# Convolution and attention kernel: another order, other engines and other buffers in the prologue

## The reference, cut to what matters

```python
def gn(v): ...  # 32 groups of 8 channels: (v - mean) / sqrt(var + 1e-5)
p = gn(x).mean((2, 3))
angle = tanh(relu(p @ ap_w1.T + ap_b1) @ ap_w2.T + ap_b2) * pi / 4
mod = sigmoid(relu(p @ meta_w1.T + meta_b1) @ meta_w2.T + meta_b2)
x = x + conv3x3(gn(x), rotate(base_kernel, angle)) * mod
t = gn(x) as tokens
q, k, v = t @ Wq.T + bq, t @ Wk.T + bk, t @ Wv.T + bv
q, k = focus((relu(q) + 1e-6) / softplus(scale)), the same of k  # cubes with the norm kept
out = q (k.T v) / (q . sum k) + dwconv5x5(v) + dwc_b           # per head
x = x + out @ Wproj.T + bproj
```

## Time and profile before

| what | us |
|---|---|
| median of three runs | 3972.8 |
| the profiled execution | 3968.21 |
| its span (first to last instruction) | 3966.1 |
| TensorE busy in the span | 3555.9 (90%) |
| VectorE, ScalarE, GpSimd busy | 2978.9, 2704.6, 1425.3 |
| first convolution starts on TensorE | 113.67 |
| second convolution starts on TensorE | 198.11 |
| first `squares` of the loop over images | 286.17 |

### The profile page before, as it was taken

The page is one execution under the profiler, slowest core; times in us unless marked ns, Lnnn a source line. Parts: engine busy times, 40 slices in busy tenths (PEclk is TensorE's granted clock), DMA queues, the critical chain, the costliest instruction groups (busy, mean ns, idle before and its releaser), DMA issues.

```text
span 3966.1 us, 96093 instructions
## 1 busy us (share of the span) xinstructions
PE 3555.9 (90%) x27980; PEld 2859.5 (72%) x27980; DVE 2978.9 (75%) x8235; ACT 2704.6 (68%) x7348; POOL 1425.3 (36%) x1318
## 2 busy tenths in 40 slices
PE   0569989999999999999999998999999899999797
PEld 0138777777877777777777877777787777778686
DVE  6766877868778786877868687786868778585756
ACT  2247776776777677677766767776677767677675
POOL 4532442514334252433525243351424425140302
PEclk9989999999999999999999999999999999999999
DMA  4672634536354452635436263443636344260302
GB/s 156 202 236 65 173 98 143 161 90 186 109 155 116 131 173 82 184 112 149 130 111 192 71 184 113 138 141 108 179 91 178 99 145 132 79 181 22 102 17 75
DMA packets 560047, 516.42 MB, mean 130 GB/s; under 512 B 97600, under 2 KB 491968, under 8 KB 559552
## 3 DMA queue, kind: packets, MB, share of 16 engines
q1 hardware_dynamic: 555200, 508.99, 43.4%
q10 hardware_dynamic: 4352, 1.57, 0.2%
HBM read 351.06 MB, written 134.22 MB: 122 GB/s over the span
## 4 chain that ended last, share of the span: by engine, by line
PE 34%; DVE 29%; issue 17%; ACT 14%; DVEq 2%; DMA 1%; ACTq 1%; SPq 1%; POOL 1%; POOLq 0%
PE F L1557 7%; ACT K L1295 6%; PE VAB L1557 6%; PE F L1518 6%; PE VAB L1518 5%; PE T L1529 4%; DVE F L975 3%; DVE XR L1064 3%; ACT K L1301 3%; DVE XR L1057 3%; DVE XHL L969 3%; DVE K L981 2%; DVE XR L1046 2%; DVE RATIO L989 2%; PE PP L1608 2%
## 5 line engine op out<-in xcount | busy, mean ns | idle before, releaser
L1518 PE MATMUL F<-WQ,XHL 128*128 128x256 f16 x6144 | 819.3, 274 | 27.7 <-ACT V L1335 19.1
L650 POOL TENSOR_TENSOR XR<-XR,V 128x512 f32<-128x512 f32 x256 | 325.6, 1272 | 1042.9 <-DVE XR L1046 1042.9
L1518 PEld LDWEIGHTS F<-WQ,XHL 128*128 128x128 f16 (+1 forms) x6144 | 602.2, 99 | 106.8 <-issue 33.9
L1301 ACT ACTIVATE K<-K,SCAL 128x256 f32<-128x256 f32 x1024 | 512.4, 505 | 209.2 <-DVE K L981 208.2
L634 POOL TENSOR_TENSOR SL<-PL,SL 128x1122 f16<-128x1122 f32 x112 | 259.7, 2319 | 1065.2 <-DVE SL L947 1065.2
L1504 PE MATMUL SM<-SL,BD 128*128 128x512 f16 x2688 | 634.9, 385 | 0.0
L1295 ACT ACTIVATE K<-F,SCAL 128x256 f32<-128x256 f32 x1024 | 473.4, 469 | 232.0 <-DVE F L975 231.6
L975 DVE TENSOR_TENSOR F<-F,FL 128x512 f32<-128x512 f32 x512 | 354.1, 692 | 176.7 <-PE F L1520 175.4
L981 DVE TENSOR_TENSOR K<-K,F 128x512 f32<-128x512 f32 x512 | 349.3, 682 | 167.2 <-ACT K L1295 166.6
L1504 PEld LDWEIGHTS SM<-SL,BD 128*128 128x128 f16 x2688 | 261.0, 97 | 284.1
L1608 PE MATMUL PP<-XR,WP 128*128 128x256 f16 x3072 | 385.6, 276 | 67.8 <-DVE XR L1064 67.8
(11 more groups left out here) (194 smaller groups left out, 6948.0 us busy)
## 6 DMA issues: line engine op xcount, KB each, us to landing
XR<-xr SPq DMA_DIRECT2D x132, 512.0 KB, 5.2
U<-x SPq DMA_DIRECT2D x256, 256.0 KB, 3.8
XR<-x SPq DMA_DIRECT2D x256, 256.0 KB, 4.1
out<-XR SPq DMA_DIRECT2D x256, 256.0 KB, 3.8
PL<-xp SPq DMA_DIRECT2D x112, 561.0 KB, 3.8
RX<-xr SPq DMA_DIRECT2D x118, 512.0 KB, 4.2
x<-RX SPq DMA_DIRECT2D x448, 128.0 KB, 2.1
BD<-RX SPq DMA_DIRECT2D x240, 96.0 KB, 2.2
```

The lines of the kernel that those rows point to most:

```text
L650: g_.tensor_tensor(o, o, fm, ALU.add).then_inc(o_rdy, 2)
L1301: a.activation(K2[:, p, t * C:(t + 1) * C], K3[:, p, t * C:(t + 1) * C], ACT.Square, scale=inv_a, accum_out=S6[:, 2 * p + t:2 * p + t + 1] ...
L1518: t_.matmul(o, XHL[:, xa, h, at], WQ[:, wa, h, c0:c0 + C], start=(k == 0), stop=False)
```

## The change

- **SP's order**: the pixels of image 0 first, then the convolution's constants, then planes, the scale, four tiles of image 1, and only then the taps' scalars and the attention's weights. `load_stats(2, 0)` and `(2, 1)` move ahead of the first convolution.
- **VectorE's order**: statistics of image 0 first; softplus after `high(0, 0..2)`; the largest weights, biases and scales after the angle of image 1. `ready` is raised at the end of that.
- **Largest values**: instead of the `partition_all_reduce`, `largest(k)` runs twice: a transpose on TensorE, a reduction, a diagonal, a second matmul, a copy. `largest(1)` stands ahead of the first `convolve` in TensorE's order.
- **Taps**: three buffers (PL, and SL twice) in place of four; ScalarE writes the high half and then the scaled value back (two activations a chunk); GpSimd subtracts. Three chunks before the first convolution, none in it, one in every round g of the second (`load_taps(g + 3)`, `taps(g + 3)`, `low_taps(g + 3)`) and one behind it. TensorE's wait for all chunks moves to the depthwise part of image 0.
- **Weights**: the high halves are four activations on ScalarE ahead of `planes(0, 3)`; VectorE makes the low halves with one operation each in place of three.
- **`rotation(1)`** has `conv_low(0, 7)` inside it, after step 8, and not behind it.

```diff
         def taps_tile(i):
-            return U2[:, i % 2, :] if i % 4 < 2 else KS[:, i % 2, :]
+            return PL[:, 0:PIX] if i % 3 == 0 else SL[:, i % 3 - 1]...bitcast(f32)[:, 0:PIX]
...
             def load_taps(i):
-                if i >= 4:
-                    sp.wait_ge(tp_dve, i - 3)
+                if i >= 3:
+                    sp.wait_ge(tp_rdy, i - 2)
                     carry(sp)
...
             def first_convolution():
                 for g in range(GROUPS):
-                    if g < 4:
-                        load_taps(2 * g + 4)
-                        load_taps(2 * g + 5)
                     store_x1(0, g)
...
             def second_convolution():
...
-                sp.wait_ge(tp_dve, CHUNKS)
-                carry(sp)
-                for g in (0, 1):
-                    load_stats(2, g)
...
                 for g in range(GROUPS):
+                    load_taps(g + 3)
                     store_x1(1, g)
...
+                load_taps(CHUNKS - 1)
+                sp.wait_ge(tp_rdy, CHUNKS)
+                carry(sp)
...
+            def low_taps(i):                       # GpSimd
+                pool.wait_ge(tp_act, 2 * i + 2)
+                carry(pool)
+                hi, lo = (TPM[:, 8 * i:8 * i + 8, a, :] for a in range(2))
+                g_.tensor_tensor(lo, taps_tile(i).rearrange("p (m n) -> p m n", m=8), hi, ALU.subtract
+                                 ).then_inc(tp_rdy, 1)
...
-            pool.wait_ge(set_dve, 1)
-            g_.partition_all_reduce(SCAL[:, 0:4], S6[:, 0:4], P, RMAX).then_inc(set_pool, 1)
...
-            rotation(1, lambda j: conv_low(0, 3 + j // 2) if j in (0, 2, 4, 6) else None)
-            conv_low(0, 7)
+            rotation(1, lambda j: conv_low(0, 3 + j // 2) if j % 2 == 0 else None)
             for g in range(3):
                 conv_low(1, g)
+            for i in range(3):
+                low_taps(i)
             for g in range(GROUPS):
                 if g + 3 < GROUPS:
                     conv_low(1, g + 3)
                 if g >= 4: (attn_input of units 2g - 8 and 2g - 7)
+                low_taps(g + 3)
+            low_taps(CHUNKS - 1)
...
+            def largest(k):                        # VectorE
+                dve.sem_inc(most_rdy, 1)
+                dve.wait_ge(most_mm, 2 * k + 1)
+                setup(v.tensor_reduce(TOP, PP[0:4, 0:P], AX.X, ALU.max))
+                setup(v.tensor_scalar(DIAG, MATS[0:4, 0, 0:4], TOP, None, ALU.mult))
+                dve.sem_inc(most_rdy, 1)
+                dve.wait_ge(most_mm, 2 * k + 2)
+                setup(v.tensor_copy(SCAL[:, 0:4], SM[:, 64:68]))
...
-            def split(src, hi, lo, a):
-                setup(v.tensor_scalar(src, src, a, None, ALU.mult))
-                setup(v.tensor_copy(hi, src))
-                setup(v.tensor_tensor(lo, src, hi, ALU.subtract))
+            def split(k, src, hi, lo, a):
+                dve.wait_ge(hi_rdy, k + 1)
+                setup(v.scalar_tensor_tensor(lo, src, a, hi, ALU.mult, ALU.subtract))
...
-            dve.wait_ge(w_in, 16 * N_W)
-            softplus()
-            largest_weights()
+            for g in range(GROUPS):
+                pixel_stats(0, g)
             dve.wait_ge(c_in, 16 * N_C)
             largest_kernel()
-            for g in range(GROUPS):
-                pixel_stats(0, g)
+            largest(0)
             scaled_kernels()
             (deviations, spreads, variance, tail, take_norms of image 0)
+            for g in range(4):
+                pixel_stats(1, g)
             modulation(0)
             modulation_back(0)
             for g in range(3):
                 high(0, g)
-            largest_biases()
-            scales()
-            for g in range(GROUPS):
+            dve.wait_ge(sc_in, 16)
+            softplus()
+            for g in range(4, GROUPS):
                 pixel_stats(1, g)
             (deviations, spreads, variance, tail of image 1)
-            for h in range(HALVES):
-                split(wq32[:, h, :], WQ[:, 0, h, :], WQ[:, 1, h, :], a_w)
-            for i in range(4):
-                low_taps(i)
+            largest_taps()
+            dve.wait_ge(w_in, 16 * N_W)
+            largest_weights()
+            largest(1)
+            largest_biases()
+            scales()
...
+            def taps(i):                           # ScalarE
+                act.wait_ge(taps_in[i % 3], 16 * (i // 3 + 1))
+                a.activation(TPM[:, 8 * i:8 * i + 8, 0, :], ..., ACT.Copy, scale=a_t).then_inc(tp_act, 1)
+                a.activation(taps_tile(i), taps_tile(i), ACT.Copy, scale=a_t).then_inc(tp_act, 1)
...
+            for i in range(3):
+                taps(i)
+            act.wait_ge(ready, 1)
+            for k, (hi, src, s) in enumerate(...): # wq32 twice, wp32, bq32
+                a.activation(hi, src, ACT.Copy, scale=s).then_inc(hi_rdy, 1)
...
             for g in range(GROUPS):                # ScalarE, second convolution
                 if g + 3 < GROUPS:
                     planes(1, g + 3)
                 (root(2) at g = 2, root(3) at g = 6)
                 if g:
                     shift(1, g - 1)
                 if g >= 4: (attn_input of units 2g - 8 and 2g - 7)
+                taps(g + 3)
             shift(1, GROUPS - 1)
+            taps(CHUNKS - 1)
             squash(2)
```

More of the change, by code:

```diff
@@ L255, in taps_tile @@
         def taps_tile(i):
-            return U2[:, i % 2, :] if i % 4 < 2 else KS[:, i % 2, :]
+            return PL[:, 0:PIX] if i % 3 == 0 else SL[:, i % 3 - 1].rearrange("p a n -> p (a n)").bitcast(f32)[:, 0:PIX]
         def alive(u):
@@ L539, in _ @@
                 load_stats(1, g)
-            sp.wait_ge(s0_rdy, 12)
-            carry(sp)
-            for i in range(4):
-                load_taps(i)
+            sp.dma_start(dt32, dw_taps[0, :].partition_broadcast(P)).then_inc(t_in, 16)
+            sp.dma_start(DWB[:, :], dw_b[0, :].partition_broadcast(P)).then_inc(t_in, 16)
+            sp.dma_start(wq32, wqkv.rearrange("(h p) n -> p h n", p=P)).then_inc(w_in, 16)
+            sp.dma_start(bq32, bqkv[0, :].partition_broadcast(P)).then_inc(w_in, 16)
+            sp.dma_start(wp32, wproj.rearrange("(h p) n -> p h n", p=P)).then_inc(w_in, 16)
+            sp.dma_start(BP[:, :], bproj).then_inc(w_in, 16)
+            sp.dma_start(BPC[:, :], bproj_patch).then_inc(w_in, 16)
             for g in range(4, GROUPS):
@@ L547, in _ @@
                 load_stats(1, g)
-            weights(0)
+            for i in range(3):
+                load_taps(i)
             for g in range(4):
@@ L552, in _ @@
                 load_pixels(0, g)
+            for g in (0, 1):
+                load_stats(2, g)
+            weights(0)
             first_convolution()
@@ L711, in setup @@
                 dve.wait_ge(set_chain, steps[SET])
-            for t in (ONES, BQ, KVS, HID, NOT, ST):
+            for t in (ONES, BQ, KVS, HID, NOT, ST, S6):
                 setup(v.memset(t[:], XS if t is ONES else 1.0 if t is ST else 0.0))
+            setup(v.memset(ONE4, 1.0))
             setup(v.memset(CK[:, :], HALF_PI))
@@ L805, in scales @@
                 dve.sem_inc(ready, 1)
-            def split(src, hi, lo, a):
-                setup(v.tensor_scalar(src, src, a, None, ALU.mult))
-                setup(v.tensor_copy(hi, src))
-                setup(v.tensor_tensor(lo, src, hi, ALU.subtract))
+            def split(k, src, hi, lo, a):
+                dve.wait_ge(hi_rdy, k + 1)
+                setup(v.scalar_tensor_tensor(lo, src, a, hi, ALU.mult, ALU.subtract))
             def split_bias():
-                split(bq32, bh16, bl16, a_w)
+                split(3, bq32, bh16, bl16, a_w)
                 setup(v.tensor_copy(BQ[0:1, :], bh16[0:1, :]))
                 setup(v.tensor_copy(BQ[32:33, :], bl16[32:33, :]))
[L817 to L821, removed]
             def link(k, ins):
@@ L1186, in _ @@
                         take_norms(1)
-                    if q == 1 and g == 0:
+                    if q == 1 and g < 2:
+                        split(g, wq32[:, g, :], WQ[:, 0, g, :], WQ[:, 1, g, :], a_w)
+                    if q == 1 and g == 2:
+                        split(2, wp32, WP[:, 0], WP[:, 1], a_p)
+                    if q == 1 and g == 3:
                         split_bias()
-                    if q == 1 and g == 1:
-                        split(wp32, WP[:, 0], WP[:, 1], a_p)
-                    if 2 <= g < 6:
-                        low_taps(2 * g + q)
             dve.sem_inc(ready, 1)
@@ L1400, in late_weights @@
                     weight_block(act, j)
-            exponentials()
             root(0)
@@ L1408, in _ @@
                 act.sem_inc(s, n)
-            act.wait_ge(ready, 1)
-            for i in range(4):
-                high_taps(i)
+            exponentials()
             root(1)
@@ L1414, in _ @@
             late_weights(0)
+            act.wait_ge(t_rdy, 1)
+            for i in range(3):
+                taps(i)
```

(12 more changed lines are left out.)

38 lines of the change are left out of this document (14 added, 24 removed).

## The result

The changed kernel took 3982.9 us, the median of 20 runs (3975.8 to 3994.7), and the kernel before 3972.4 in 20 runs beside them (3964.7 to 3980.9). The ratio is 1.0033, with a 95% interval of 1.0025 to 1.0041: slower by 0.33%, 10 to 16 us. The forecast was slower by 18.8 us.

What follows compares the result with a forecast made beforehand. The prologue was taken as a chain of waits, no engine full. H at 167.8 plus 137.2 puts `squares` at 305.0, 18.8 later: 3987.0 us against the profiled 3968.2, 3991.6 against the median; range 3962 to 4009.

Steps and rivals of the forecast that it cites:

- Ahead of H: Prologue up to the second convolution: VectorE's new order raises `ready` at 97.2, and H comes 30.3 us earlier.
- H: Start of the second convolution on TensorE: 198.1 us before, forecast at 167.8, with 160 to 173 as bounds.
- Being held: VectorE operations ahead of `ready` slowed beside GpSimd's rotation or `conv_low`: 0 to 16 us, 7.5 taken.
- The all-reduce: Its removal takes two pool configurations and a 7.1 us gap before the rotation away; nothing counted for it.
- From conv_low(0, 7) to H: Stores, last pixel group and weights' DMAs before the second convolution: 25.0 us, kept as before.
- Behind H: Second convolution's rounds: ScalarE waits a turn through SP and HBM for each chunk; `squares` at H + 137.2, 49.1 more.
- A1: Start of ScalarE's round 1 behind H, 20.2 us after it; A2 to A7 are the later rounds, A7 at 113.5.
- Cover: Behind H: GpSimd's twelve subtractions, about 2.1 us each, lie under ScalarE's next work; without cover up to 2 a round.
- The chunks are there when ScalarE asks: Rival for the rounds behind H: about 10 us of activations show, 3952 us; chance 0.15.
- The two cancel: Rival: no operation held, H at 160, turns at their lower end, 126, sum 286; 3973 us; chance 0.17.
- Held everywhere: Rival: GpSimd holds VectorE everywhere, H at 173, 147 behind it, sum 320; 4007 us; chance 0.06.
- nothing gained ahead: Rival: the rotation goes on setting the new order as before, H at 192; 4016 us; chance 0.02.

Runs made afterwards that it cites:

- e1: The changed kernel unedited, run and profiled a second time; median 3990.8 us, ratio 1.0038 to the kernel before.
- e9: Changed kernel with sixteen large operations of image 0's rotation on GpSimd cut to 128x18 elements; 3977.5 us, ratio 1.0017 to the kernel before.
- e7: Changed kernel with taps' chunks loaded one turn early and GpSimd's first rotation behind VectorE's three casts; 3936.4 us, ratio 0.9917 to the kernel before.
- e4: Changed kernel with the GpSimd all-reduce back for the first largest values, the second ones still on TensorE; 3981.4 us, ratio 1.0020 to the kernel before.
- e2: Changed kernel with each chunk of taps loaded one round earlier (g + 4 in round g); 3941.4 us, ratio 0.9915 to the kernel before.
- e8: Kernel before with only the taps moved as in the change, chunks 3 to 11 in the second convolution's rounds; 4020.4 us, ratio 1.0127.
- e3: Changed kernel with chunks 3 to 11 of the taps neither loaded nor split, zeros in their place; 3932.8 us, ratio 0.9890 to the kernel before.

## Why the prediction was right, and where its sizes were off

**Ahead of H.** The sum gave 17, 31.7, `ready` 97.2, `conv_low(0, 3)` ending 106.3, `conv_low(0, 7)` 142.8, H 167.8. Measured: 17.8, 32.6, 98.7, 107.5, 143.3, 166.3 (e1: 168.9). So distances between rows of before, laid end to end in the new order, met each of these points within 1.5 us. At `ready` that is in part luck, because two errors cancel:

- Being held, bounds 0 to 16, of which I took 7.5, was some 13: 9.3 us of chain from the largest kernel value to the scales that e9 took away (80.9 to 71.5) and the 3.5 that e9 kept.
- The unheld distances were some 5 too long. Image 1's chain is 10.0 without being held (image 0's in the kernel before, 38.82 to 48.78) and not 11.7, because my row began ahead of the scaling of the kernel, 1.7 us that only image 0 has. The taps' scalars, biases and scales are 10.2 and not 13.2, because the row of before already held some 2.7 of waiting beside GpSimd, which I noted and left in.

**The rule on shared interfaces.** In the trace, softplus's twelve scalings and two-input operations ran among the rotation's large operations; nine took 0.9 to 1.5 us, the other three 0.29 to 0.43, as all twelve do in e9. The reciprocals (1.75) and the statistics (4.84) kept their time beside the rotation, and so did the reductions of the weights (3.19) beside `conv_low` in e7. The Trainium skill (GPSIMD Engine Reference, section 1) names instructions with two SBUF inputs or in a 2-port mode, and the trace agrees in kind. My reading of it, some 25 operations held by 1 us each, was too much by 12: the three casts and the largest weights met no large GpSimd operation in the changed kernel, and outside softplus only a few small operations were held, the longest, beside `conv_low`, for 1.85 and 2.09 us.

**The all-reduce.** "I expect the gap to go but count nothing." The gap went. Its price was taken on the wrong side: I looked at what an earlier rotation could give (the weights' landing) and not at whom it would then run beside. e4, with the gap back, has H 6 to 9 us earlier in the profile; in the time the gain is at the edge of what can be told (1.0020 beside 1.0038 for e1, intervals overlapping).

**From conv_low(0, 7) to H** I kept 25.0; it is 23.0.

**The size of the whole.** `squares` were forecast at 305.0 and came at 310.7 and 312.4; the profiled execution at 3987.0 and was 3994.65. Against the medians the error has the other sign: 3991.6 forecast, 3982.9 measured (e1 3990.8), +18.8 forecast and +13 by the ratio. I had added the traces' difference to a median of three, as if one execution stood for all; what one execution is off by, 4 us under for before and 12 over for the changed kernel, is as large as the error of any term. Against the difference of the traces, +24.5, the sum of +18.8 is 6 too low, against the ratio's +13 it is 6 too high; that it lies between them is no merit of its terms.

**Behind H.** The mechanism, a turn through SP and HBM in every round with the next round queued behind it, is shown: by the waits' names, by e2, which takes only the turns away and with them 49 us, and by e8, which has them alone. The term was mis-sized by 7 us: 137.2 forecast, 144.3 measured (e1 143.6). Starts of the rounds behind H, forecast and measured: A1 20.2 and 20.5, A2 34.3 and 36.8, A3 52.3 and 55.8, A4 64.5 and 68.0, A5 82.9 and 87.3, A6 98.1 and 103.5, A7 113.5 and 120.9. Two terms account for most of the 7.4 at A7. Round 1's chunk landed 11.9 after the shift's end where I had 9.3 (2.6), and round 2's 13.1 where I had 12 (1.1). And the lone chunk of rounds 4 to 6, for which I took 4.0 from issue to landing by the earlier trace rows, took 4.75, 4.96 and 6.1 (246.78 to 251.53, 262.77 to 267.73, 279.07 to 285.14), 3.8 in all: it is issued right behind four loads of a quarter MB for the units, and the row I took it from had no such loads right in front of it.

**Cover.** e2 has all subtractions and activations and is 49 us shorter; with the turns gone nine chunks together cost 10.7 us (e2 less e3), though they keep ScalarE busy for 18.6 us (52.1 for 33.4 in e3) and GpSimd for 19.0. What the subtractions add by themselves no run shows; it is at most these 10.7.

**The rivals.** "The chunks are there when ScalarE asks" is what e2 makes true: I gave it 3952 in the changed kernel, and e2 measured 3941; its 10 us for the chunks that show are the 10.7 above. "The two cancel" was nearest after the forecast: the measured +10 to +16 lies between it and +18.8. "Held everywhere" put H at 173 and "nothing gained ahead" at 192; both are excluded by H, though being held, at 13, was nearer to the first one's 16 than to my 7.5.

## What to carry to other kernels

When a load is moved into a round, look at what its issue is queued behind: if that is a store which waits for the same engine that will wait for the load, each round pays a whole turn, and one line that issues it a round earlier is worth more (49 us here) than all that the change won ahead (32). When a chain is re-ordered, lay measured distances end to end in the new order; that met H within 1.5 us over 150, here with two errors of 5 us that cancelled, so look at what a row taken over already contains. An idle gap on one engine may shelter another: before removing it, ask what will then run side by side.

## What the runs showed of the hardware

- GpSimd's 128x576 operations stretched VectorE's 128x256 operations from 0.29 to as much as 1.41 us (scalings, 0.87 to 1.41) and from 0.42 to 1.1 to 1.5 us (two inputs). How much differs from run to run: the same six operations took 2.7, 3.8 and 9.2 us in three executions.
- A 15.46 us memset on GpSimd held a 4x4 scaling on VectorE for 4.23 us, until near its end at 23.07.
- Behind an all-reduce and a MODIFY_POOL_CONFIG GpSimd's first two-input operation came 9.2 us after the latter in e4 (34.2 to 43.41) and 7.1 in the kernel before (52.6 to 59.70); without an all-reduce it came 0.24 after its releaser, ScalarE's sine (36.28 to 36.52). The Trainium skill (GPSIMD Engine Reference, section 2.1) gives the load of code as approximately 6 us; both of these gaps are longer.
- TensorE's granted clock behind H was on average 0.71 of full speed (2.4 GHz) in the changed kernel, 0.84 before and 0.80 in e2, so each of these stretches ran in part at the lower level of 1.2 GHz; TensorE idled 74, 29 and 31 us of these stretches. What the lower clock costs was not measured apart; it can lie only in the 70 of 144 us in which TensorE works.
